# A transformer block kernel rewritten so that weights arrive as stationary tiles: no weight transposes, the residual in the attention matrix, down products in groups

## What is computed

```
xn = layernorm(x)
attn = (lin(xn, Wq) + lin(xn, Wk) + lin(xn, Wv)) / 3      # NF4 codes x scales, each with a rank-16 LoRA
x1 = xn + lin(attn, Wo)
s  = x1 + lin(silu(lin(x1, G)) * lin(x1, U), D)           # NF4 + LoRA; G, U: 1792 x 512, D: 512 x 1792
W' = mean_w + mean(|w - mean_w|) * sign(w - mean_w)       # for w1, w2, w3
g  = silu((silu(xn W1'^T) * (xn W3'^T)) W2'^T)
out = x + s * g
```

## Time and profile before

| | |
|---|---|
| median of 3 runs | 634.94 us (633.91 to 636.35) |
| span of the profiled execution | 632.0 us |
| TensorE busy | 584.8 us (93%), 2794 matmuls |
| Vector busy | 487.1 us (77%) |
| ACT busy | 348.1 us (55%) |
| POOL busy | 157.4 us (25%) |
| DMA | 63.09 MB, mean 100 GB/s |

### The profile page before, as it was taken

The page is one execution under the profiler, slowest core; times in us unless marked ns, Lnnn a source line. Parts: engine busy times, 40 slices in busy tenths (PEclk is TensorE's granted clock), DMA queues, the critical chain, the costliest instruction groups (busy, mean ns, idle before and its releaser), DMA issues.

```text
span 632.0 us, 8467 instructions
## 1 busy us (share of the span) xinstructions
PE 584.8 (93%) x2794; PEld 480.9 (76%) x2794; DVE 487.1 (77%) x569; ACT 348.1 (55%) x447; POOL 157.4 (25%) x110
## 2 busy tenths in 40 slices
PE   0698799998999899999999899999999999999993
PEld 0577678886878788888678688888888888888883
DVE  5956776498999999889674488887878888887347
ACT  2547562464655537576443585776848577583210
POOL 3413206543343452210120011011111011111005
PEclk9989899998999999999999999999999999999998
DMA  8798748324333331100730011020111101100303
GB/s 339 305 398 304 200 135 239 114 97 165 100 128 95 95 114 50 51 1 5 158 134 1 0 52 51 11 65 24 50 50 50 50 0 50 50 0 15 118 1 133
DMA packets 56964, 63.09 MB, mean 100 GB/s; under 512 B 15216, under 2 KB 36720, under 8 KB 56944
## 3 DMA queue, kind: packets, MB, share of 16 engines
q1 hardware_dynamic: 56944, 62.84, 30.4%
HBM read 60.73 MB, written 2.10 MB: 99 GB/s over the span
## 4 chain that ended last, share of the span: by engine, by line
PE 71%; DVE 12%; issue 7%; ACT 5%; DMA 2%; POOL 2%; SPq 1%; POOLq 0%; DVEq 0%; ACTq 0%
PE gate_ps L1416 16%; PE up_ps L1416 16%; PE sum_ps L1437 10%; PE tr_ps L1294 5%; PE up_ps L1437 4%; PE gate_ps L1437 4%; PE sum_ps L1590 4%; PE up_ps L1335 3%; DVE weight L1000 3%; PE tr_ps L1398 2%; DVE attn_sum L1040 1%; PE gate_ps L1346 1%; DVE y L923 1%; DMA y<-L_attn_x 1%; ACT ramp L668 1%
## 5 line engine op out<-in xcount | busy, mean ns | idle before, releaser
L1416 PE MATMUL up_ps<-xT,guT 128*128 128x512 f32 x576 | 138.4, 393 | 0.0
L1416 PE MATMUL gate_ps<-xT,guT 128*128 128x512 f32 x576 | 138.4, 393 | 0.0
L1031 DVE SCALAR_TENSOR_TENSOR base<-ramp,base 128x1536 f32<-128x1536 f32 x70 | 122.6, 1752 | 3.6 <-ACT ramp L658 2.1
L1416 PEld LDWEIGHTS up_ps<-xT,guT 128*128 128x128 f32 x576 | 107.0, 188 | 21.5
L1416 PEld LDWEIGHTS gate_ps<-xT,guT 128*128 128x128 f32 x576 | 107.0, 188 | 21.5
L658 ACT ACTIVATE ramp<-raw,ramp_bias 128x1536 f32<-128x1536 int32 x70 | 108.9, 1577 | 0.0
L440 POOL TENSOR_TENSOR weight<-base,scale_trio 128x1536 f32<-128x1536 f32 x14 | 38.7, 2767 | 244.6 <-DVE base L1031 244.6
L1437 PE MATMUL sum_ps<-downT,h_split 128*128 128x512 f32 x288 | 72.1, 400 | 5.1 <-DVE h_split L1021 5.1
L1437 PEld LDWEIGHTS sum_ps<-downT,h_split 128*128 128x128 f32 x288 | 54.3, 192 | 17.3 <-issue 6.4
L627 ACT ACTIVATE guT<-tr_ps 128x512 fp32r<-128x512 f32 x48 | 28.7, 597 | 64.8 <-PE tr_ps L1398 37.2
L639 ACT ACTIVATE h_split<-up_ps 128x512 fp32r<-128x512 f32 x48 | 28.7, 598 | 64.6 <-DVE up_ps L1014 64.6
(11 more groups left out here) (192 smaller groups left out, 798.7 us busy)
## 6 DMA issues: line engine op xcount, KB each, us to landing
raw<-L_ffn_w SPq DMA_DIRECT2D x42, 256.0 KB, 3.6
base<-L_ffn_mean_w SPq DMA_DIRECT2D x42, 256.0 KB, 4.9
scan<-L_ffn_w SPq DMA_DIRECT2D x12, 640.0 KB, 7.8
scan<-L_ffn_mean_w SPq DMA_DIRECT2D x12, 640.0 KB, 8.9
raw<-L_attn_codes_gu SPq DMA_DIRECT2D x14, 512.0 KB, 3.7
attn_codes<-L_attn_codes_attn SPq DMA_DIRECT2D x4, 1024.0 KB, 4.7
raw<-L_attn_codes_down SPq DMA_DIRECT2D x14, 256.0 KB, 3.9
y<-L_attn_x SPq DMA_DIRECT2D x2, 1024.0 KB, 6.5
```

The costliest lines, as they stand in the source:

```text
L1031: nc.vector.scalar_tensor_tensor(base[:, par, :], ramp[:, (step % 2) * TRIO:(step % 2 + 1) * TRIO], NF4_RAMPS[j][2], base[:, par, :], ALU. ...
L1416: last = nc.tensor.matmul(ps, guT[:, par, kind, w_part, hc * P:(hc + 1) * P], xT[:, x_part, hc, th * HALF:(th + 1) * HALF], start=(hc == 0 ...
```

## The change

The kernel is written anew around tiles that the host lays out. Before the launch the host cuts the weights, means and codes into the stationary form, so that a tile of gate or up has input features as rows; scales of block 1 come as rows that a DMA broadcasts to 64 partitions each; x is given a second time transposed, and the output is stored transposed. The names of the changed kernel:

- `phase(k)`: chunk k (0 to 13 block 0, 14 to 27 block 1) on one engine; `down_stage(g)`: the down product of a group of two to four chunks (`GROUPS`), now with the down tile stationary and h moving, 8 tiles of 4 output parts x 2 token halves, through three PSUM banks. A group has one y add per tile, so there are 10 x 8 in place of 14 x 8.
- `before_stage(m)`: the split of the weights of chunk m + 2 from SBUF (`weight_high`, `weight_low`: 1024 + 512 columns), and sign and make of chunk m + 3. `ffn_make` and `ffn_subtract` as before.
- Attention steps s = 0 to 39 (`attn_step`) go by half tiles of codes a = s // 5 through one buffer `attn_acc` (1024 columns): at the first step of each half ACT writes its start value, after the fifth POOL works on it (`attn_qk` or `attn_vo`). `ATTN_STEPS` says in which stage each step stands ("D1": in down stage 1). The same steps carry small Vector operations for the matmuls `lora_qkv`, `lora_o` (4 each) and `fold` (16 x 3), which stand between other matmuls of TensorE and share one PSUM bank, `side_ps`; `side_used` counts its six uses per tile. `fold` adds the product of both attention matrices to `MT_acc`, which starts as the identity, so the residual is in M.
- In block 1 the LoRA of gate and up is one matmul of 96 rows per product on a table T made once from x1 (`T3`), the LoRA of down one matmul (`lora_down`) that Vector adds to the weights. The steps of block 1 alternate two accumulators.
- x1 M goes straight to transposed x1 (no transposes); down stage 4 comes after it.

```diff
+GROUPS = [(0, 1, 2, 3), (4, 5, 6), (7, 8, 9), (10, 11), (12, 13),
+          (14, 15, 16), (17, 18, 19), (20, 21, 22), (23, 24, 25), (26, 27)]
...
+ATTN_STEPS = {"D0": range(0, 8), 4: range(8, 11), 5: range(11, 14), 6: range(14, 17), "D1": range(17, 25),
+              7: range(25, 28), 8: range(28, 31), 9: range(31, 34), "D2": range(34, 40), 10: range(40, 45),
+              11: range(45, 49)}
...
+    def project_tiles(w):
+        return w.reshape(CHUNKS, P, HC, P).transpose(0, 3, 2, 1).reshape(CHUNKS, P, HID)
+    def down_tiles(w):
+        return w.T.reshape(CHUNKS, P, HID)
...
+        "scale_qkv": scales_attn[0:3].reshape(3, HC, P, 8).transpose(2, 1, 0, 3),
...
+                for c in range(HC):
+                    nc.gpsimd.tensor_copy(MT_acc[:, c, c * P:(c + 1) * P], ident[:]).then_inc(MT_zero, 1)
...
+            def B_down_low():
+                pool.wait_ge(table_hi, 3)
+                pool.wait_ge(attn_pool, 15)
+                nc.gpsimd.tensor_tensor(B_down[64:96, :], table_raw[64:96, 0:HID], B_down[64:96, :].bitcast(f32),
+                                        ALU.subtract).then_inc(table_lo, 1)
...
+            ffn_subtract(5)
+            ffn_subtract(6)
+            attn_qk(0)
+            attn_vo(0)
+            ffn_subtract(7)
+            ffn_subtract(8)
+            attn_qk(1)
+            A_down_low()
+            ffn_subtract(9)
+            attn_vo(1)
+            attn_qk(2)
+            ffn_subtract(10)
+            attn_vo(2)
+            B_down_low()
+            ffn_subtract(11)
...
+            def attn_step(s):
...
+                    if j == 0:
+                        act.wait_ge(attn_loaded, 16 * a + 16)
+                        if a == 0:
+                            act.wait_ge(dn_lo, 2)
+                        else:
+                            act.wait_ge(attn_pool, 5 * (a // 2) + (2 if a % 2 else 0))
+                        nc.scalar.activation(attn_acc[:, :, :], attn_codes[:, :, :].bitcast(i32), ACT.Copy,
+                                             bias=NF4_START, scale=NF4_STEP).then_inc(attn_start, 1)
...
+            def before_stage(m):
+                if m + 2 < 2 * CHUNKS:
+                    weight_high(m + 2)
+                if FIRST < m + 3 < CHUNKS:
+                    ffn_signs(m + 3)
...
+            h_high(3, 0)
+            attn_table_high()
+            h_high(3, 1)
...
+            phase(7)
+            phase(8)
+            act.wait_ge(table_loaded[1], 32)
+            nc.scalar.activation(B_down[0:ROWS3, :], table_raw[0:ROWS3, 0:HID], ACT.Copy).then_inc(table_hi, 1)
...
+            def weight_low(k):
+                src = base if k < B0 else acc
+                if k >= B0:
+                    dve.wait_ge(nf4_scaled, k - B0 + 1)
+                    dve.wait_ge(side_done, 24 + k - B0 + 1)
+                    nc.vector.tensor_tensor(acc[:, k % 2, 2 * HID:], acc[:, k % 2, 2 * HID:], side_ps[:, :], ALU.add
+                                            ).then_inc(side_used, 1)
+                dve.wait_ge(gu_hi, gu_count(k))
+                nc.vector.tensor_tensor(gu[:, k % 2, :, LO, :], src[:, k % 2, 0:2 * HID].rearrange("p (m n) -> p m n", m=2),
+                                        gu[:, k % 2, :, HI, :].bitcast(f32), ALU.subtract).then_inc(gu_lo, 1)
+                dve.wait_ge(dn_hi, k + 1)
+                nc.vector.tensor_tensor(dn[:, k % DN_SLOTS, LO, :], src[:, k % 2, 2 * HID:],
+                                        dn[:, k % DN_SLOTS, HI, :].bitcast(f32), ALU.subtract).then_inc(dn_lo, 1)
...
+            def attn_step(s):
...
+                    dve.wait_ge(attn_ramped, s + 1)
+                    if j > 0:
+                        dve.wait_ge(attn_added, s)
+                    nc.vector.scalar_tensor_tensor(attn_acc[:, :, :], attn_ramp[:, s % 2, :, :], NF4_RAMPS[j][2],
+                                                   attn_acc[:, :, :], ALU.min, ALU.add).then_inc(attn_added, 1)
+                mi, at = (s - 11) // 10, (s - 11) % 10
+                if not 0 <= mi < 4:
+                    return
+                if at == 0:
+                    dve.wait_ge(attn_pool, 5 * mi + 5)
+                    dve.wait_ge(side_done, 6 * mi + 1)
+                    nc.vector.tensor_tensor(w_qkv32[:, LO, :], w_qkv32[:, LO, :], side_ps[:, :], ALU.add
+                                            ).then_inc(side_used, 1)
+                if at == 1:
+                    dve.wait_ge(side_done, 6 * mi + 2)
...
+                if 4 <= at < 8:
+                    hc = at - 4
+                    dve.wait_ge(side_done, 6 * mi + 3 + hc)
+                    if mi == 0 and hc == 0:
+                        dve.wait_ge(MT_zero, 1 + HC)
+                    nc.vector.tensor_tensor(MT_acc[:, hc, :], MT_acc[:, hc, :], side_ps[:, :], ALU.add
+                                            ).then_inc(side_used, 1)
...
+            def before_stage(m):
+                if m + 2 < 2 * CHUNKS:
+                    weight_low(m + 2)
+                if FIRST < m + 3 < CHUNKS:
+                    ffn_make(m + 3)
+            def phase(k):
+                if PLACE_OF[k] > 0:
+                    before_stage(k - 1)
+                background(k, 0, 2)
+                h_make(k, 0)
+                background(k, 2, 3)
+                h_low(k, 0)
+                h_make(k, 1)
+                background(k, 3, 12)
+                h_low(k, 1)
...
+            h_low(3, 1)
+            y_tile(0, 0)
+            ffn_make(4)
+            y_tile(0, 1)
+            weight_low(4)
+            y_tile(0, 2)
+            ffn_make(5)
+            background("D0", 0, 1)
+            y_tile(0, 3)
+            background("D0", 1, 2)
+            for t in range(4, TT):
+                y_tile(0, t)
+                background("D0", t - 2, t - 1)
+            ffn_make(6)
+            background("D0", TT - 2, 12)
+            weight_low(5)
+            for g in (1, 2, 3):
+                for k in GROUPS[g]:
+                    phase(k)
+                down_stage(g)
+            phase(12)
+            phase(13)
+            for c in range(HC):
+                dve.wait_ge(MT_hi, c + 1)
+                nc.vector.tensor_tensor(MT[:, LO, c, :], MT_acc[:, c, :], MT[:, HI, c, :].bitcast(f32), ALU.subtract
+                                        ).then_inc(MT_lo, 1)
+            before_stage(13)
...
-            def unit(block_no, c, par, kind):
-                index = unit_index(block_no, c, kind)
-                bank = (3 * par + kind) % 2
-                pe.wait_ge(w_hi, index - 1)
-                pe.wait_ge(w_lo, index - 1)
-                if block_no == 0:
-                    pe.wait_ge(ffn_weight, index + 1)
-                else:
-                    pe.wait_ge(nf4_weight, c + 1)
-                last = transpose4(tr_ps[:, bank, :], lambda n: weight[:, par, kind * HID + n * P:kind * HID + (n + 1) * P],
-                                  accumulate=block_no == 1)
-                if block_no == 1 and kind == DOWN:
-                    pe.wait_ge(A_down_ready, c + 1)
-                    last = nc.tensor.matmul(tr_ps[:, bank, :], A_down_now[:, par, :], B_downT[:, :],
-                                            start=False, stop=True)
-                elif block_no == 1:
-                    for n in range(HC):
-                        last = nc.tensor.matmul(tr_ps[:, bank, n * P:(n + 1) * P], A_gu[:, kind, n * P:(n + 1) * P],
-                                                B_guT[:, ds(c * P, P)], start=False, stop=(n == HC - 1))
-                last.then_inc(tr_done, 1)
...
+            def project(k, kind, th):
...
+                if k >= B0:
+                    pe.wait_ge(T_lo, th + 1)
+                    pe.wait_ge(table_lo, 5)
+                    c = k - B0
+                    last = nc.tensor.matmul(ps[:, :], B_gu[0:ROWS3, kind, c * P:(c + 1) * P],
+                                            T3[0:ROWS3, th * HALF:(th + 1) * HALF], start=False, stop=True)
...
+            def down(g, t):
...
+                elif n >= 3:
+                    pe.wait_ge(y_done, n - 2)
+                for k in ks:
+                    for w_part, h_p in PASSES:
+                        last = nc.tensor.matmul(down_ps[n % 3][:, :], dn[:, k % DN_SLOTS, w_part, hq * P:(hq + 1) * P],
+                                                h_part(k, h_p, th), start=(k == ks[0] and w_part == h_p == HI),
+                                                stop=(k == ks[-1] and w_part == LO))
+                last.then_inc(down_done, 1)
...
+            def lora_o(mi):
+                pe.wait_ge(side_used, 6 * mi + 1)
+                nc.tensor.matmul(side_ps[:, :], A_o[:, mi * P:(mi + 1) * P], B_o[:, :], start=True, stop=True
+                                 ).then_inc(side_done, 1)
+            def fold(mi, hc):
+                pe.wait_ge(attn_lo, 2 * mi + 2)
+                pe.wait_ge(side_used, 6 * mi + 2 + hc)
+                for a_part, b_part in PASSES:
```

(61 more changed lines are left out.)

2087 lines of the change are left out of this document (898 added, 1189 removed).

## The result

The changed kernel takes 787.3 us (785.3 to 789.0) against 634.95: a ratio of 1.240 (1.236 to 1.244). I had forecast slower, at 682, and the range ended at 708. The direction was right, the size was not: 152 us more instead of 47. By the traces block 0 took 236.1 us in the kernel before and 320.2 now, block 1 299.7 and 364.3: 84 us of the loss lie in block 0 and 65 in block 1. I had forecast 59 and 1.

A forecast was written before the change was run, and what follows sets the result against it. TensorE was taken as the bound, Vector close behind. Start 91.0, matmuls 188.2 and 282.0, waits 106.9 and 14.4, end 3.9 gave a span of 686.4, so 689; with 667 as alternative, 682 us was taken, range 636 to 708.

The forecast's parts named there:

- TensorE's work: Matmuls at full clock: 188.2 us from first down product to product with M, 282.0 us after it.
- Start: Before the first down product: first coefficient at 34.3, first projection at 36.4, first down product at 91.0 us.
- Block 0's waits: TensorE's waits between first down product and product with M, listed by chunk and down stage, sum 106.9 us.
- my walk: Going through each engine's instruction list by hand with priced operations to find TensorE's waits; it gave a span of 686.4 us.
- My walk adds every lateness up, and it is nearer: Choice between 689 us from the walk and 667: nearer to 689, so 682 us was taken.
- the waits priced alone: Waits of chunks 5 and 9 without earlier lateness, 6.2, 9.3 and 6.5 us less, giving 667 us.
- Block 1 has few holes, since its accumulator is doubled: Block 1: only 14.4 us of waits, 4.5 in down stage 4 and 3.7, 3.7, 2.5 in stages 5 to 7.
- The rule against the change: POOL and Vector operations with two SBUF inputs exclude each other; 40 steps and 10 makes cost Vector 19 us more.
- Vector's total: Rival: Vector's 203 us of work in block 0 is the limit, holes are filled; faster, 620 us, chance 0.15.
- Slower still: Rival: 19 us from the exclusion rule, or 3.1 us of low clock after each of six waits; 707 us, chance 0.10.
- What was to show it: Signs named beforehand: TensorE's busy share per block, fold and lora_o idle time, chunk 9's wait, times of first down product and M.

The follow-up runs named there:

- f3: The changed kernel with 370 matmuls that nobody reads added where TensorE waited longest: 784.0 us.
- e7: The changed kernel with the attention ramps and steps cut to 16 of 1024 columns on ACT and Vector: 751.3 us.
- e2: The changed kernel with ACT's third and fourth ramp of a stage ahead of both high parts of h from chunk 12 on: 747.0 us.
- e3: The changed kernel with POOL's scaling of block 1's weights cut to 8 of 1536 columns: 763.1 us.
- f4: Vector, not POOL, scales block 1's weights, against a 735.6 us kernel with ACT's ramps ahead everywhere and POOL's down-table low parts later: 731.7 us.

## Why the prediction was wrong

- **TensorE's work** (188.2 and 282.0): the counts hold (831 and 1244 matmuls in the windows, for 830 and 1244). TensorE was busy 27 and 26 us longer than at full clock, and that cost nothing (f3). The saving on transposes, 19 us in block 1, buys nothing here: f3 gave TensorE 78 us more to do, and no stretch grew.
- **Start** 91.0, was 99.0, and 97.5 to 103.3 in the other runs. The first coefficient, which I had put at 34.3 without a sum behind it, came at 36.09, and so the first projection began at 38.48, not 36.4; the waits were 2.94, 3.50 and 3.75 us before the last gate and two of the up projections. Vector's normalising took 12.63 us, 9.87 in the kernel before; whether that delayed the coefficient was not tested.
- **Block 0's waits**, 106.9, were 105.2, near place by place (chunk 5 5.8 and 18.6 for 6.2 and 17.6, chunk 6 12.1 for 10.4, chunk 9 21.5 for 19.4; too high in down stage 2, 6.7 for 10.8, too low before M, 12.2 for 6.8). That the sums agree is in good part luck. The term that the forecast needs is 132.0, all time over TensorE's work at full clock, and it was 25 us too low. And the cause was half wrong: in chunk 5 the longest hole was a transfer, which my walk did not have, in the place of POOL's 3.9 and a later start of the steps, and with the steps cut to 16 columns 75 us of idle time stayed (e7). "My walk adds every lateness up, and it is nearer" holds so far as the waits priced alone (667) lay further off, and taking 682 between the two was a choice against my own argument. Where the 25 us come from stays open: other orders shorten block 0 (ACT's ramps 4.0, POOL's list 6.4, the place of two matmuls 11.2), but my walk had the lists as they stood.
- **The step that failed: "Block 1 has few holes, since its accumulator is doubled".** I counted 14.4 us of waits there, and the stretch came out 64 us longer than its sum (364.3 for 300.3). I looked for holes of the accumulator and summed Vector's durations; the order of ACT's list, in which a ramp stands behind a high part that waits for Vector's make, I had in front of me and priced as "a step of 1.58 + 1.75 between the parts of h", once, against TensorE's 3.2, and not as what makes Vector wait 63 us over the block. Moving two ramps of a stage on ACT takes away 36 of the 64 (e2), cutting POOL's scaling 17 (e3, on the change as it was). How much of the 17 is left behind e2 was only tried by f4's exchange, which gave nothing, and what else keeps block 1 at 328, 46 us over TensorE's work at full clock, stays open.
- **The rule against the change.** I gave 19 us for it in block 0 and left it to a rival. What it takes of Vector's time is read from the means of the steps over their short values: 40 x (1.447 - 1.22) = 9.1 and 70 x (2.062 - 1.75) = 21.8 us. The makes, for which I had 12 of the 19, took 0.80 each and not 1.15. In the kernel before block 1's steps had 1.75: each fifth step there is followed on Vector by operations with a PSUM operand, while POOL scales (POOL 373.67 to 376.44, the next step at 376.78). The change puts a step directly behind the fifth, and where the two met it, issued 1.48 us into 3.43 us of scaling, took 1.80 us longer than its 1.76. The Trainium skill, SBUF — State Buffer, "SBUF: two separate sides", says that GpSimd (POOL) and a Vector operation with two SBUF inputs share a pair of ports, and that the one that starts first keeps it for its whole instruction. By that rule the step should be 1.95 us late, so this trace agrees to 0.15.
- **Rivals.** Vector's total (194 us busy of 320 in block 0, my sum had 203) was not the limit. "Slower still" at 707 had the right sign but two mechanisms of which one, the low clock, costs nothing, and the other lies mostly in block 1's steps (21.8 of 30.9), where I had not put it. What came was none of my cases: a chance for "block 1 also waits" was missing, and with it the range.
- **What was to show it**: PE below 70% in block 0 (67%), idle before fold and lora_o of 74 us (40 or more), chunk 9 over 8 us: right. PE near 100% in block 1 (84%), the first down product near 91 (99), M near 380 (419), 300 from it to the end (364): wrong.

## What to carry over

When two engines hand each other a buffer, walk both lists side by side: an operation whose inputs are ready stands still behind one that waits for the other engine, and here this cost 36 us in one block. Ramps that need only old inputs belong ahead of the operations that wait. Where a helper engine locks another out, as POOL's scaling did with Vector's steps, let it run beside operations that it doesn't lock out; a new order can lose that without one instruction more or less. Before charging a low clock, ask who waits for the matmuls. And a sum of waits that agrees is no proof of their causes: cut the work that is said to cause them, and look what stays.

## What the runs showed of the hardware

- The granted clock was 0.77 in the mean from 128 to 225 us of the changed kernel. After a wait of 5.81 us it was 0.52, the lower of its two levels (1.2 GHz): there twelve matmuls of 512 columns took 5.41 us, where twenty-four take 5.44 at the upper one. With filler the same kernel ran at 0.94 in the mean, in the same time.
- A Vector step of 1.76 us that met POOL's scaling took 3.56, and 4.68 where it was issued 0.4 us into it; both end 1.6 us after POOL.

```profile
531.34 3.50 POOL L522 TENSOR_TENSOR acc<-acc,scale 128x1536 f32<-128x1536 f32 x1 [18.74 <-DVE acc L995]
531.77 4.68 DVE L995 SCALAR_TENSOR_TENSOR acc<-ramp,acc 128x1536 f32<-128x1536 f32 x1
```

- Even operations of 8 columns are locked out: in the start, one of Vector's operations on 128x8 operands took 2.24 us where its neighbours took 0.17, beside a POOL subtract of 2.34 us that had begun 0.11 us earlier; both ended within 0.01 us of each other.
- POOL's scaling by a full 128x1536 operand took 3.48 us, by broadcast scales 2.77 in the kernel before.
